# Attention in a three-layer kernel: the PSUM banks for maxima and exponentials, and the order of their products

## The reference

```
xd = (layernorm(x) @ W_down).reshape(b, t, 16, 16)
keys, queries, values = einsum(xd, tokeys), einsum(xd, toqueries), einsum(xd, tovalues)   # keys, queries scaled
attn = softmax(queries . keys)          # 16 heads of 16 features, 1024 x 1024 each
x = x + (attn @ values) @ W_unify + b_unify
```

## Time and profile before

| | |
|---|---|
| median of 3 runs | 2732.42 us (2726.8 to 2734.16) |
| profiled execution, its own time | 2731.22 us |
| its span in the profile | 2729.5 us |
| PE, DVE, ACT, POOL busy | 96%, 74%, 65%, 34% |
| mean granted clock of TensorE | 0.979 |
| first maximum to last exponential of attention | 618.6 to 2139.8 us |

### The profile page before, as it was taken

One profiled execution on the slowest core, in us unless ns is written; L12 is line 12 of the kernel. 1 busy time (PEld: TensorE's weight loads), 2 busy tenths in 40 slices (PEclk: granted clock), 3 DMA queues, 4 the chain that ended last, 5 costly groups with the idle time before them and its releaser, 6 DMA issues. The chain is left out here.

```text
span 2729.5 us, 45612 instructions
## 1 busy us (share of the span) xinstructions
PE 2627.3 (96%) x17009; PEld 1574.4 (58%) x17009; DVE 2021.7 (74%) x3407; ACT 1761.2 (65%) x3314; POOL 917.5 (34%) x975
## 2 busy tenths in 40 slices
PE   6999999968999999999999999999999699999998
PEld 5888899953334334333343343343333388888998
DVE  5656547848898898897988988978997266665586
ACT  4444456734787887877877878878778344444576
POOL 2333334641332242423323322422212133332364
PEclk9999999986999999999999999999999699999999
DMA  4421214515144243242342442432421331321253
GB/s 116 100 70 56 62 52 137 156 53 101 48 85 85 55 96 66 65 99 52 77 105 51 90 80 54 81 65 65 84 68 32 107 86 57 76 70 32 86 160 96
DMA packets 191805, 216.79 MB, mean 79 GB/s; under 512 B 56364, under 2 KB 152804, under 8 KB 191584
## 3 DMA queue, kind: packets, MB, share of 16 engines
q1 hardware_dynamic: 156176, 169.03, 26.6%
q0 software_dynamic: 35408, 44.84, 5.8%
HBM read 114.54 MB, written 48.57 MB: 60 GB/s over the span
## 5 line engine op out<-in xcount | busy, mean ns | idle before, releaser
L1383 DVE TENSOR_REDUCE at_mxc<-at_pb 128x2 f32<-128x1024 f32 x1024 | 1217.7, 1222 | 185.2 <-PE at_pb L1208 178.4
L1316 ACT ACTIVATE at_ex<-at_pd 128x512 f32<-128x512 f32 x2048 | 1074.1, 603 | 328.9 <-PE at_pd L1219 325.1
L1219 PE MATMUL at_pd<-at_qa,at_ka 50*128 50x512 f32 x2048 | 616.2, 471 | 4.4 <-ACT at_ex L1316 4.4
L1219 PEld LDWEIGHTS at_pd<-at_qa,at_ka 50*128 50x128 f32 x2048 | 271.2, 186 | 570.8 <-issue 410.2
L699 ACT ACTIVATE f_ml_h<-f_ml_pL,b1T 128x512 f32<-128x512 f32 (+1 forms) x384 | 243.2, 633 | 480.2 <-PE f_ml_pL L763 458.7
L1228 PE MATMUL at_po<-at_ex,at_va 128*32 128x512 f32 x4096 | 551.5, 611 | 0.0
L614 DVE TENSOR_TENSOR f_ml_hl<-f_ml_h,f_ml_hh 128x512 fp32r<-128x512 f32 (+1 forms) x384 | 277.9, 724 | 368.0 <-ACT f_ml_hh L702 335.1
L1208 PE MATMUL at_pb<-at_ka,at_qa 48*128 48x512 f32 x2048 | 412.0, 447 | 21.6 <-DMA at_ka<-at_parts 11.3
L776 PE MATMUL f_ml_pA<-f_wh,f_ml_hh 128*128 128x256 f32 (+1 forms) x1408 | 411.4, 292 | 0.0
L778 PE MATMUL f_ml_pA<-f_wl,f_ml_hh 128*128 128x256 f32 (+1 forms) x1408 | 396.8, 282 | 0.0
L779 PE MATMUL f_ml_pA<-f_wh,f_ml_hl 128*128 128x256 f32 (+1 forms) x1408 | 396.7, 282 | 0.0
(11 more groups left out here) (123 smaller groups left out, 2642.0 us busy)
## 6 DMA issues: line engine op xcount, KB each, us to landing
f_wraw<-in_L_ffn_w SPq DMA_DIRECT2D x128, 256.0 KB, 2.9
at_qa<-at_parts SPq DMA_DIRECT2D x384, 64.0 KB, 2.5
at_ka<-at_parts SPq DMA_DIRECT2D x384, 64.0 KB, 2.7
at_oscr<-at_os POOLq DMA_DIRECT2D x63, 256.0 KB, 2.4
f_ml_xr<-in_L_attn_x SPq DMA_DIRECT2D x16, 512.0 KB
f_ml_xs<-in_L_attn_x SPq DMA_DIRECT2D x16, 512.0 KB, 4.6
x<-f_ml_yo SPq DMA_DIRECT2D x16, 512.0 KB, 6.2
at_xr<-x SPq DMA_DIRECT2D x16, 512.0 KB, 5.3
```

Of the source, the lines that this page charges most:

```text
L1219: eng.matmul(pd[n % RING][:, :], ka[g][rows, p, kt * P:(kt + 1) * P], qa[g][rows, qh, p, :], start=True, stop=True).then_inc(s_full.sem, 1)
L1316: eng.activation(ex[t % 2][:, j, :], pd[n % RING][:, :], ACT.Exp).then_inc(s_free[n % RING].sem, 1)
L1383: eng.tensor_reduce(mxc[:, t // NT, kh, t % NT::NT], pb[kh][:, :].rearrange("p (e k) -> p e k", e=2), AX.X, ALU.max, negate=True).then_inc ...
```

## The change

The ring `pd` gets a fourth bank. The maxima get a ring of three single banks in place of two tiles of two; each head's 512 columns are a tile of their own, with a product, a wait and a TENSOR_REDUCE each (four in a step in place of two, 2048 in place of 1024). Tile n waits for the reduction of tile n - 3. The exp products are issued in the order 1, 0, 3, 2, and the step on TensorE is: max e0, exp 1, exp 0, max e1, side product, max e0, exp 3, exp 2, max e1, times_v. The banks are eight before and after (4 + 3 + 1).

```diff
-RING = 3
+RING = 4
+MRING = 3
+ORDER = (1, 0, 3, 2)
...
-        pb = [ps(f"pb{i}", [P, T]) for i in range(2)]
+        pb = ps("pb", [P, MRING * 512])
...
+        def tile_of_max(b, g, t, kh, e):
+            return 4 * (ST * unit(b, g) + t) + 2 * kh + e
+
+        def bank_of_max(n):
+            return pb[:, n % MRING * 512:(n % MRING + 1) * 512]
...
-                eng.wait_ge(s_mx.sem, s_mx.at(2 * (ST * unit(b, g) + t) + kh - 1))
-                for e in range(2):
-                    rows = slice(HALF * e, HALF * e + KROWS)
-                    mm = eng.matmul(pb[kh][:, e * NQ:(e + 1) * NQ], qa[g][rows, qh, p, qt * P:(qt + 1) * P],
-                                    ka[g][rows, p, kh * NQ:(kh + 1) * NQ], start=True, stop=True)
-                mm.then_inc(s_b.sem, 1)
+                n = tile_of_max(b, g, t, kh, e)
+                eng.wait_ge(s_mx.sem, s_mx.at(n - MRING + 1))
+                rows = slice(HALF * e, HALF * e + KROWS)
+                eng.matmul(bank_of_max(n), qa[g][rows, qh, p, qt * P:(qt + 1) * P],
+                           ka[g][rows, p, kh * NQ:(kh + 1) * NQ], start=True, stop=True).then_inc(s_b.sem, 1)
...
 TensorE, step
-                    for j in range(2 if tiles else 0):
-                        for_exp(self.ring, *coming, j, tiles[j])
-                    if ahead:
-                        for_max(*ahead, 0)
-                    if a:
-                        side_product(self.ring, a)
-                    if ahead:
-                        for_max(*ahead, 1)
-                    for j in range(2, GH if tiles else 2):
-                        for_exp(self.ring, *coming, j, tiles[j])
+                    for kh in range(2):
+                        if ahead:
+                            for_max(*ahead, kh, 0)
+                        for i in (2 * kh, 2 * kh + 1) if tiles else ():
+                            for_exp(self.ring, *coming, ORDER[i], tiles[i])
+                        if ahead:
+                            for_max(*ahead, kh, 1)
+                        if a and kh == 0:
+                            side_product(self.ring, a)
                     times_v(self.ring, b, par, g, t, done)
...
 VectorE
-            def maximum(b, g, t, kh):
-                eng.wait_ge(s_b.sem, s_b.at(2 * (ST * unit(b, g) + t) + kh + 1))
-                eng.tensor_reduce(mxc[:, t // NT, kh, t % NT::NT], pb[kh][:, :].rearrange("p (e k) -> p e k", e=2),
+            def maximum(b, g, t, kh, e):
+                n, c = tile_of_max(b, g, t, kh, e), t % NT + NT * e
+                eng.wait_ge(s_b.sem, s_b.at(n + 1))
+                eng.tensor_reduce(mxc[:, t // NT, kh, c:c + 1], bank_of_max(n),
                                   AX.X, ALU.max, negate=True).then_inc(s_mx.sem, 1)
...
-                    if ahead:
-                        maximum(*ahead, 0)
+                    for e in range(2 if ahead else 0):
+                        maximum(*ahead, 0, e)
...
+                    for e in range(2 if ahead else 0):
+                        maximum(*ahead, 1, e)
                     if ahead:
-                        maximum(*ahead, 1)
```

More of the change, by code:

```diff
@@ L965, in attention @@
         norm = Norm(ctx, nc, k, "at_ln_", NT)
-        pb = [ps(f"pb{i}", [P, T]) for i in range(2)]
+        pb = ps("pb", [P, MRING * 512])
         pd = [ps(f"pd{i}", [P, 512]) for i in range(RING)]
         po = ps("po", [P, 512])
-        diagonals = Diagonals(ctx, nc, w, k, pb[0], xres[:, :, :])
+        diagonals = Diagonals(ctx, nc, w, k, pb[:, 0:2 * 512], xres[:, :, :])
         S = lambda n: Sem(ctx, nc, "at_" + n)
@@ L1198, in _, with for_max @@
                 s.open(eng)
-            def for_max(b, g, t, kh):
+            def for_max(b, g, t, kh, e):
                 qh, p, qt = t // NT, t % NT // 4, t % 4
-                if kh == 0 and (t == 0 or g == 0 and t == NT // 2):
+                if kh == 0 and e == 0 and (t == 0 or g == 0 and t == NT // 2):
                     eng.wait_ge(landed(g, p).sem, landed(g, p).at(loads(g, b + 1)))
-                eng.wait_ge(s_mx.sem, s_mx.at(2 * (ST * unit(b, g) + t) + kh - 1))
-                for e in range(2):
-                    rows = slice(HALF * e, HALF * e + KROWS)
-                    mm = eng.matmul(pb[kh][:, e * NQ:(e + 1) * NQ], qa[g][rows, qh, p, qt * P:(qt + 1) * P],
-                                    ka[g][rows, p, kh * NQ:(kh + 1) * NQ], start=True, stop=True)
-                mm.then_inc(s_b.sem, 1)
+                n = tile_of_max(b, g, t, kh, e)
[3 more added lines that the diff above has]
+                           ka[g][rows, p, kh * NQ:(kh + 1) * NQ], start=True, stop=True).then_inc(s_b.sem, 1)
             def for_exp(ring, b, g, t, j, n):
                 qh, kt, e, p = t // NT, t % NT, j % 2, j // 2
-                if kt == 0 and j == 0:
+                if kt == 0 and j == ORDER[0]:
                     eng.wait_ge(s_mr[qh].sem, s_mr[qh].at(16 * MLOADS * (unit(b, g) + 1)))
@@ L1283, in first @@
                         for kh in range(2):
-                            for_max(0, 0, t, kh)
+                            for e in range(2):
+                                for_max(0, 0, t, kh, e)
                 def lead(self, b, g, tiles):
-                    for j, n in enumerate(tiles):
+                    for j, n in zip(ORDER, tiles):
                         for_exp(self.ring, b, g, 0, j, n)
                 def step(self, b, par, g, t, coming, tiles, done, a, side, ahead, last):
-                    for j in range(2 if tiles else 0):
-                        for_exp(self.ring, *coming, j, tiles[j])
-                    if ahead:
-                        for_max(*ahead, 0)
-                    if a:
-                        side_product(self.ring, a)
-                    if ahead:
-                        for_max(*ahead, 1)
-                    for j in range(2, GH if tiles else 2):
-                        for_exp(self.ring, *coming, j, tiles[j])
+                    for kh in range(2):
[7 more added lines that the diff above has]
+                            side_product(self.ring, a)
                     times_v(self.ring, b, par, g, t, done)
@@ L1355, in lead @@
                 def lead(self, b, g, tiles):
-                    for j, n in enumerate(tiles):
+                    for j, n in zip(ORDER, tiles):
                         exponentials(self.ring, 0, j, n)
                 def step(self, b, par, g, t, coming, tiles, done, a, side, ahead, last):
-                    for j in range(2 if tiles else 0):
-                        exponentials(self.ring, t + 1, j, tiles[j])
+                    for i in (0, 1) if tiles else ():
+                        exponentials(self.ring, t + 1, ORDER[i], tiles[i])
                     if a:
                         side_out(self.ring, a)
-                    for j in range(2, GH if tiles else 2):
-                        exponentials(self.ring, t + 1, j, tiles[j])
+                    for i in (2, 3) if tiles else ():
+                        exponentials(self.ring, t + 1, ORDER[i], tiles[i])
                     if t % NT == NT - 1:
@@ L1388, in both_halves @@
                 h = half(b, g, qh)
-                eng.wait_ge(s_mx.sem, s_mx.at(2 * (ST * unit(b, g) + NT * (qh + 1))))
+                eng.wait_ge(s_mx.sem, s_mx.at(4 * (ST * unit(b, g) + NT * (qh + 1))))
                 eng.tensor_reduce(nm[:, qh, :], mxc[:, qh, :, :].rearrange("p k c -> p c k"), AX.X,
@@ L1476, in first @@
                         for kh in range(2):
-                            maximum(0, 0, t, kh)
+                            for e in range(2):
+                                maximum(0, 0, t, kh, e)
                         if t % NT == NT - 1:
```

## The result

The changed kernel takes 2741.98 us, the median of 5 runs (2741.39 to 2746.23), against 2731.75 (2724.33 to 2734.16) for the kernel before: ratio over all runs 1.0049, 95% interval 1.0031 to 1.0066 (that of the two medians alone is 1.0037). It is slower by about half a per cent. The prediction was 2751 with a range of 2734 to 2766: the direction is right, the sum 9 us too high. The profiled execution took 2746.2 us (span 2744.5), the slowest of the five, 4 us above their median; before, the profiled one was within 1 us of its median.

What follows compares the result with a forecast made beforehand. The bound was taken to be the ring of three banks through ScalarE, not TensorE's or VectorE's work. Terms 31 + 8 - 10 - 1 + 2 - 11 = +19 on 2731.2 gave 2750, as median 2751 us, range 2734 to 2766.

Steps and rivals of the forecast that it cites:

- (a): Ring of four: the fourth exp product's bank wait goes; TensorE of itself would need 2.24 us a step.
- (c): Maxima in three single banks: the fourth max product waits for the first one's 688 ns reduction, making the step 2.71 us.
- rivals 1 and 2: Maxima loop: reduction costs half (611 ns), total 2720, chance 0.09; or the ring closes no loop, total 2650, chance 0.06.
- (d): VectorE's total: four reductions, 2.40 us, fit a 2.71 us step; small operations push the next reductions, together +8 us.
- (e): Plain steps: 308 go from 2.61 to 2.71 us, +31; 50 following a values copy stay at 2.71.
- (f): Side steps: projections 0; 56 transpose steps save 0.18 us each, -10; values copies in some side steps, -1.
- (g): The start: 26 reductions at 1.13 us become 52 at 0.60, +2 us.
- (h): Tail, 11 steps without maxima: the old loop opens, -15 us if the clock stays, -9 if it falls; -11 taken.
- Rival 3: TensorE's clock falls to half in plain steps: loop 4.17 us, +520 us if in all, total 3270; chance 0.03.

Runs made afterwards that it cites:

- banks dealt the other way: The changed kernel with four single banks for maxima and three for exp and side products: 2735.72 us, ratio to before 1.0012.
- order alone: The kernel before with only the new order of products (1024-column reductions, ring of three kept): 2727.73 us, ratio 0.9997.
- half the reduction: The changed kernel with each reduction reading 256 of its 512 columns: 2636.47 us, ratio to before 0.9667.
- tail alone: The kernel before with only the last 13 steps' exp and side products going round seven banks: 2719.11 us, ratio to before 0.9949.

## Why the prediction was right

(a), (c) The loop. It was to be 2.71 us: 0.54 to 0.55, 0.69, 0.05, 0.43, 1.00. It is 2.70, with 0.54, 0.69, 0.05, 0.43, 0.99. The unknown price, 688 ns from two lengths of the same operation, measures 683. That it came within 5 ns is in part luck: the 188 ns row reads SBUF, not PSUM, and gives 16 results a partition. With the runs there are three lengths that read PSUM, 419 ns for 256 columns, 683 for 512 and 1222 for 1024, so 1.03 and 1.05 ns a column. The Trainium skill's rule (VectorE: DVE Perf Modes, "The TRN2 errata") gives 658 for it as an estimate; the trace is 25 ns above, as it was 30 above at 1024 columns. The experiments with two banks, half the columns and the old order move the step as the loop says (+0.6, -0.26, +0.47), and rivals 1 and 2 are out: the reduction did not halve, and the wait does close the loop.

(d) The pushes of the small operations. Predicted +8. In the profile after, 207 undisturbed plain steps take 2.70 and 54 take longer, 2.8 to 3.1 for most: 7.9 us together above 2.70; 41 of the 54 are steps t = 3 and t = 11, right behind the two dependent operations, as expected. Steps around a values copy (2.79, then 2.64, by the start of the exponential) cancel but for 1 us: there the copy moves where the exponential starts, not the loop.

(e), (f) Plain steps with the pushes +38.1, predicted +39; transposes -10.3, predicted -10 and -0.7; projections 0.3, predicted 0 and -0.7.

(g) The start: +2.1, predicted +2.

(h) The tail: -14.4, predicted -11. This is the one term that was mis-sized. I had hedged between a clock that stays (-15) and one that falls; it stayed. Only the first side product still waits, 2.2 us, for GpSimd's divisions. The size of this gain is a matter of the execution, too: with the clock up through all 11 steps the old tail would take 28.7 us, an estimate from its first five (2.60 to 2.61, one of 2.70 with a values copy), and the gain would be 6 us in place of 14.

The sum of what was predicted, +19, stands against +16.7 in attention: the tail saved 3 us more than predicted and the plain steps cost 1 less, and the last step's 1.6, which waits for the divisions, was not in it. The remaining difference between 2751 and 2742 is outside: the rest of the span was 1.7 us shorter in the profiled execution, and that execution lies 4 us above its median, so that comparing the profiles gives +15.0 and the medians +10.2. Runs of one kernel spread by 2 to 18 us here; a forecast in single microseconds from one profile cannot be better than that. The spread has a pattern. The kernels whose profiled tail fell to half clock (before, banks dealt the other way, order alone) spread by 12 to 18 us in 10 to 22 runs each, those whose tail stayed up (changed, half the reduction, tail alone) by 2 to 6 in 4 to 6 runs each. In 22 runs of the kernel before the time goes with the mean granted clock, from 2718.6 us at 0.984 to 2733 to 2736 at 0.975 and 0.976. That it is the tail in which these runs differ is likely, but not shown: there is a profile of one execution of each kernel only.

Rival 3, the clock: it stayed at 1.00 in the middle of the stage, with a wait of 0.52 us in each step where 0.42 stood before, so for the middle of the stage the rival is out. The Trainium skill tells of a kernel that cycles through banks, idles briefly and often, and swings between both clocks (TensorE: Matmul & The Clock Gate, "A second HAM failure mode: psum-queue depth-cycling"). The middle of the stage does not agree with it; the tail of the kernel before agrees in part: there a short wait for a bank in each 2.60 us step was followed by a fall to 0.50, once, and not by a swing. The prediction gave the tale little for the plain steps and was right there; it is nearer to the tail, which the prediction took from rows.

## What to carry to other kernels

Where an engine issues k tiles of a kind in a fixed order between two long blocks, and has k - 1 banks for them, the last tile waits for the first one's reader within the same period, and the period is product + reader + block, as long as no engine's own work in a period is longer; taking a bank from another ring only hands the loop to it. Compare the two readers' latencies before dealing banks: here ScalarE's 0.60 was better placed in that loop than VectorE's 0.68. And look for stretches in which banks stand empty, such as the drained end of a pipeline: using them took no more work of any engine and gained 13 us, where the change in the middle of the stage lost 38 us in the plain steps to win 10 in the transposes.

## What the runs showed of the hardware that was not expected

The granted clock of the tail went with the ring. Without max products, the old ring (2.60 us a step, TensorE waiting for one exponential in each) went to a granted 0.50 in all three profiles that have it: after five steps in the kernel before, after three with the banks dealt the other way, after eight with the order alone. From there a step took 4.07. With seven banks (1.96 us a step, 0.22 of wait ahead of V) it stayed at 1.00 for the 11 steps, and so it did with four banks in the changed kernel and its three variants with four (2.07 us a step). So the freed wait was paid twice: 0.65 us a step directly, and 2.1 us a step for those that had run at half clock. Why the same steps fell after three, five or eight stays open.

An exp product that is the second of its pair lets its exponential start 0.57 us after the pair's start, against 0.53 where it is first (1501.64 to 1502.21, and 1517.28 to 1517.81 in the earlier trace rows); in a closed loop this alone was 0.04 a step. In the kernel before with the new order the same place cost only 0.01 (0.54). Why it differs between the two stays open.
